# Two routed expert layers: routing work spread over more units and a third weight buffer in the first, the last layer's routing of two chunks moved one turn forward

## The reference, cut to what matters

```
# layer 0, feed-forward
n = layer_norm(x); x1 = x + n + (n @ mix_w + mix_b)
flat = layer_norm(x1); probs = softmax(flat @ router_w)        # 8 experts
topw, topi = top_k(probs, 2)
h = silu(flat @ w1[e] + b1[e]); y = h @ w2[e] + b2[e]          # e in the token's two experts
x = x1 + topw[0]*y[topi[0]] + topw[1]*y[topi[1]]

# layer 3, attention with one head
att = q @ w_in + (q * dot_scale) @ memory.T - 1e30 * mask
x = x + softmax(att) @ memory                                  # q = layernorm(x)

# layer 3, feed-forward
logits = xn @ Wg.T; top_v, top_i = top_k(logits, 2); gates = softmax(top_v)
pos = cumsum(onehot(top_i)) - 1; keep = pos < cap              # cap = 1280 per expert
inp, gate = split(xn @ W1[e]); out = (gelu(inp) * gate) @ W2[e]
x = x + the kept, gated sum of the token's two experts
```

## Time and profile before

| | us |
|---|---|
| median of 3 runs (lowest to highest) | 1486.42 (1482.06 to 1490.42) |
| the profiled execution's own time | 1486.32 |
| its span | 1484.5 |
| PE / DVE / ACT / POOL busy | 1184.3 / 991.8 / 667.6 / 537.8 |

### The profile page before, as it was taken

One profiled execution on the slowest core, in us unless ns is written; L12 is line 12 of the kernel. 1 busy time (PEld: TensorE's weight loads), 2 busy tenths in 40 slices (PEclk: granted clock), 3 DMA queues, 4 the chain that ended last, 5 costly groups with the idle time before them and its releaser, 6 DMA issues. The chain is left out here.

```text
span 1484.5 us, 34946 instructions
## 1 busy us (share of the span) xinstructions
PE 1184.3 (80%) x11154; PEld 926.2 (62%) x11154; DVE 991.8 (67%) x2920; ACT 667.6 (45%) x1423; POOL 537.8 (36%) x590
## 2 busy tenths in 40 slices
PE   2799994349899957789987879999799956399991
PEld 1577773238799934566674456677477746389991
DVE  3699885564533346989974678889477777756552
ACT  1377771115455503346554546666243343144440
POOL 2323302663305256635411233431121124752554
PEclk9999995559999966889988989999799988599996
DMA  7887733012223248534532086674200042133442
GB/s 179 211 212 196 186 105 127 29 51 65 78 79 106 85 119 205 135 100 130 155 91 51 19 191 157 152 170 106 85 1 0 0 150 64 54 119 107 147 141 74
DMA packets 138979, 164.58 MB, mean 111 GB/s; under 512 B 15309, under 2 KB 118755, under 8 KB 131729
## 3 DMA queue, kind: packets, MB, share of 16 engines
q1 hardware_dynamic: 130664, 146.62, 36.7%
q0 software_dynamic: 8192, 16.46, 4.0%
HBM read 111.98 MB, written 51.38 MB: 110 GB/s over the span
## 5 line engine op out<-in xcount | busy, mean ns | idle before, releaser
L586 DVE TENSOR_REDUCE A_neg_max<-A_s_bank 128x4 f32<-128x512 f32 x384 | 253.4, 688 | 45.0 <-PE A_s_bank L725 34.5
L448 ACT ACTIVATE A_probsT<-A_st_bank 128x512 f32<-128x512 f32 x384 | 222.2, 602 | 37.9 <-PE A_st_bank L738 36.9
L725 PE MATMUL A_s_bank<-A_k_stack,A_q_stack 72*128 72x128 bf16 x1536 | 158.9, 229 | 37.3 <-DVE A_neg_max L586 23.6
L738 PE MATMUL A_st_bank<-A_q_stack,A_k_stack 128*128 128x128 bf16 x1536 | 153.4, 224 | 7.0 <-DVE A_q_stack L602 6.2
L738 PEld LDWEIGHTS A_st_bank<-A_q_stack,A_k_stack 128*128 128x128 bf16 x1536 | 113.0, 104 | 51.7 <-issue 42.3
L725 PEld LDWEIGHTS A_s_bank<-A_k_stack,A_q_stack 72*128 72x128 bf16 x1536 | 107.2, 102 | 51.7 <-DVE A_neg_max L586 34.1
L752 PE MATMUL A_pv_bank<-A_probsT,A_v_pad 128*32 128x128 f32 x3072 | 128.3, 285 | 0.1
L2043 ACT ACTIVATE E_h<-E_h_bank,w_L_b 128x256 f32<-128x256 f32 x184 | 77.0, 472 | 82.0 <-PE E_h_bank L2143 80.8
L2143 PE MATMUL E_h_bank<-E_xT,E_w_u 128*128 128x256 f32 x368 | 91.4, 394 | 6.1 <-issue 6.1
L2155 PE MATMUL E_y_bank<-E_w,E_h 128*128 x736 | 90.3, 276 | 2.2 <-ACT E_h L2043 1.0
L752 PEld LDWEIGHTS A_pv_bank<-A_probsT,A_v_pad 128*32 128x32 f32 x3072 | 74.6, 111 | 23.5 <-issue 2.2
(11 more groups left out here) (371 smaller groups left out, 2658.5 us busy)
## 6 DMA issues: line engine op xcount, KB each, us to landing
A_q_stack<-q_scratch SPq DMA_DIRECT2D x48, 576.0 KB
A_k_stack<-k_scratch SPq DMA_DIRECT2D x32, 576.0 KB
q_scratch<-A_q_parts SPq DMA_DIRECT2D x48, 192.0 KB
A_k_stack<-k_scratch SPq DMA_DIRECT2D x48, 192.0 KB
E_xe<-slots_in SPq DMA_DIRECT2D x53, 128.0 KB
slots_out<-E_ye SPq DMA_DIRECT2D x53, 128.0 KB, 1.7
A_ctxT<-in_ctxT SPq DMA_DIRECT2D x24, 256.0 KB, 10.0
k_scratch<-A_k_parts SPq DMA_DIRECT2D x32, 192.0 KB
```

Of the source, the lines that this page charges most:

```text
L448: act.activation(probsT[n % 2][:, c * HQ:(c + 1) * HQ, :], st_bank[c % 2][:, :].rearrange("k (a q) -> k a q", a=HQ), ACT.Exp, scale=scale) ...
L586: dve.tensor_reduce(neg_max[:, c * HQ:(c + 1) * HQ], s_bank[c % 2][:, :].rearrange("q (a k) -> q a k", a=HQ), AX.X, ALU.max, negate=True). ...
L725: last = pe.matmul(s_bank[c % 2][:, a * S:(a + 1) * S], q_stack[slot][0:COMBO, h, at:at + S], k_stack[slot][0:COMBO, h, at:at + S], start= ...
L738: last = pe.matmul(dst, k_stack[slot][:, h, at:at + S], q_stack[slot][:, h, at:at + S], start=True, stop=spread)
```

## The change

`routed_ffn` (layer 0):

```diff
-    LAG = 9
+    LAG = 10
+    WBUF = 3
...
-            scatter(2, 0, 8)
+            scatter(2, 0, 12)
             inverse_deviation(3)
-            scatter(2, 8, 2 * RT)
+            scatter(2, 12, 2 * RT)
...
-                if u >= 2:
-                    dve.wait_ge(h_ready, 2 * (u - 1))
-                dve.tensor_copy(w1_u[u % 2][:, :], ...)
+                if u >= WBUF:
+                    dve.wait_ge(h_ready, 2 * (u - WBUF + 1))
+                dve.tensor_copy(w1_u[u % WBUF][:, :], ...)
...
-                    expert = {0: copy_w1(0), 1: copy_w1(1)}
+                    expert = {u: copy_w1(u) for u in range(WBUF)}
...
-                    if since == 4:
-                        add_x1(2 * c)
-                        normalise(2 * c)
-                        add_x1(2 * c + 1)
-                        normalise(2 * c + 1)
+                    if since in (4, 5):
+                        add_x1(2 * c + since - 4)
+                        normalise(2 * c + since - 4)
...
-                if u == BEGIN[NR - 1] + LAG + 1:
-                    table(1)
-                    out_rows(0)
-                if u == BEGIN[NR - 1] + LAG + 2:
-                    out_rows(1)
-                if u == BEGIN[NR - 1] + LAG + 12:
-                    out_rows(2)
-                if u == BEGIN[NR - 1] + LAG + 13:
-                    out_rows(3)
+                located = u - BEGIN[NR - 1] - LAG
+                if located in (1, 2, 3):
+                    table(1, (located - 1,))
+                if located in (4, 5, 10, 11):
+                    out_rows((4, 5, 10, 11).index(located))
```

`OneHeadFront` hooks of `capacity_ffn` (layer 3):

```diff
 POOL
-                    if b in (2, RT):
-                        inverse_root(2 if b == 2 else 3)
+                    if b in (RT, RT + 2):
+                        inverse_root(2 if b == RT else 3)
 DVE
+                if (g, half) == (3, 1):
+                    choose(0)
                 if (g, half) == (4, 0):
-                    choose(0)
+                    locate(0)
                 if (g, half) == (4, 1):
+                    dve.wait_ge(layer.x_added, START + g + 1)
                     normalise(1)
-                if (g, half) == (5, 0):
-                    locate(0)
-                if (g, half) == (6, 0):
+                if (g, half) == (5, 1):
                     choose(1)
                 if (g, half) == (6, 1):
                     dve.wait_ge(layer.x_added, START + g + 1)
+                    locate(1)
...
             statistics(3)
-            locate(1)
 ACT
-                if g in (2, 5):
+                if g in (2, 4):
                     for at in ((0, 1) if g == 2 else (2, 3)):
                         copy_xn(at)
 PE
                 if (g, half) == (3, 0):
                     logits(0)
-                if (g, half) == (3, 1):
                     logits(1)
-                if (g, half) == (4, 1):
+                if (g, half) == (4, 0):
                     count(0)
...
-                if (g, half) == (6, 1):
+                if (g, half) == (6, 0):
                     pe.wait_ge(index_done, 1)
                     count(1)
```

More of the change, by code:

```diff
@@ L1588, in routed_ffn @@
         xT = [sb(f"xT{i}", [D, UT]) for i in range(3)]
-        w1_u = [sb(f"w1_u{i}", [D, FC * 128]) for i in range(2)]
+        w1_u = [sb(f"w1_u{i}", [D, FC * 128]) for i in range(WBUF)]
         h = [sb(f"h{i}", [128, FC, UT]) for i in range(2)]
@@ L1844, in locate, with table @@
                 dve.tensor_copy(index[:, :, chunk(c)], slot[:, :, chunk(c)]).then_inc(index_done, 1)
-            def table(p):
+            def table(p, pieces=(0, 1, 2)):
                 first, last = PARTS[p]
@@ L1853, in table @@
                 hit = passed[:, 0:n, :]
[L1854 to L1881, removed]
@@ L1882, in table @@
-                dve.sem_inc(table_done, 1)
+                if 0 in pieces:
+                    own.link(dve.tensor_tensor(held[:, :], base[:, last, :], begins[:, p, :], ALU.subtract))
+                    own.did(dve.tensor_scalar(lim[:, :], held[:, :], -float(UT), 0.0, ALU.add, ALU.max))
+                    own.link(dve.tensor_tensor(square[:, :, :], held[:, :, None].to_broadcast([S, NE, MOST]),
+                                               steps[:, None, :].to_broadcast([S, NE, MOST]), ALU.is_gt))
+                    own.link(dve.tensor_reduce(units[:, :], square[:, :, :], AX.X, ALU.add))
+                    own.link(dve.tensor_tensor(square[:, :, 0:NE], upto[:, :, :],
+                                               units[:, None, :].to_broadcast([S, NE, NE]), ALU.mult))
+                    own.link(dve.tensor_reduce(ends[:, :], square[:, :, 0:NE], AX.X, ALU.add))
@@ new lines, in table @@
+                if 1 in pieces:
+                    own.link(dve.tensor_tensor(hit, per_u(ends[:, :]), per_e(numbers), ALU.is_le))
+                    own.link(dve.tensor_reduce(which[:, 0:n], hit[:, :, 0:NE - 1], AX.X, ALU.add))
+                    own.link(dve.tensor_tensor(hit, hit, per_u(ends[:, :]), ALU.mult))
+                    own.link(dve.tensor_reduce(begun[:, 0:n], hit[:, :, 0:NE - 1], AX.X, ALU.max))
+                    own.did(dve.tensor_copy(expert_of[:, at:at + n], which[:, 0:n]))
+                    own.did(dve.tensor_tensor(begun[:, 0:n], numbers, begun[:, 0:n], ALU.subtract))
@@ new lines, in table @@
+                if 2 in pieces:
+                    own.link(dve.tensor_tensor(hit, per_u(core.iota8[:, :]), per_e(which[:, 0:n]), ALU.is_equal))
+                    own.link(dve.tensor_tensor(hit, hit, per_u(lim[:, :]), ALU.mult))
+                    own.link(dve.tensor_reduce(row[:, 0:n], hit, AX.X, ALU.add))
+                    own.did(dve.tensor_scalar(which[:, 0:n], which[:, 0:n], float((last - first) * REGION),
+                                              float(first * NE * REGION), ALU.mult, ALU.add))
+                    own.link(dve.scalar_tensor_tensor(row[:, 0:n], begun[:, 0:n], float(UT), row[:, 0:n], ALU.mult, ALU.min))
+                    own.link(dve.tensor_tensor(row[:, 0:n], row[:, 0:n], which[:, 0:n], ALU.add))
+                    own.link(dve.tensor_copy(row_of[:, at:at + n], row[:, 0:n]))
+                    own.did(dve.scalar_tensor_tensor(terms[:, p, 2, :], units[:, :], float(UT), lim[:, :], ALU.mult, ALU.subtract))
+                    own.did(dve.tensor_tensor(terms[:, p, 1, :], lim[:, :], begins[:, p, :], ALU.add))
+                    own.link(dve.tensor_tensor(terms[:, p, 0, :], ends[:, :], units[:, :], ALU.subtract))
+                    own.did(dve.tensor_scalar(terms[:, p, 2, :], terms[:, p, 2, :], -float(UT), None, ALU.add))
+                    own.link(dve.scalar_tensor_tensor(terms[:, p, 0, :], terms[:, p, 0, :], float(UT), begins[:, p, :],
+                                                      ALU.mult, ALU.subtract))
+                    dve.sem_inc(table_done, 1)
@@ L1966, in _ @@
                     dve.wait_ge(w1_loaded, 16 * NE)
-                    expert = {0: copy_w1(0), 1: copy_w1(1)}
+                    expert = {u: copy_w1(u) for u in range(WBUF)}
             dve.wait_ge(b2_loaded, 16)
             for u in range(last_unit):
-                if u + 2 < last_unit:
-                    expert[u + 2] = copy_w1(u + 2)
+                if u + WBUF < last_unit:
+                    expert[u + WBUF] = copy_w1(u + WBUF)
                 copy_y(u, expert[u])
```

18 lines of the change are left out of this document (9 added, 9 removed).

## The result

The changed kernel takes 1473.23 us (median of 5 runs, 1468.89 to 1477.83), the kernel before 1486.42 beside it: a ratio of 0.9917 [0.9889, 0.9945], 13.2 us less. Forecast was 1473.0.

The account below looks back on a forecast made before the run. PE was taken to bound the last layer's units, POOL's scatters their start, and DVE's extras to stall PE in the first layer. First layer -9.3 and last layer -4.1 give -13.4 from 1486.4: 1473.0 us, range 1468 to 1481.

Parts of the forecast that it names:

- gap at unit 12 with its slow clock: First layer: PE's 6.0 us wait for DVE's weight copy and 1.7 us of slow clock both go, -7.7 us.
- turn_r, unit 4's result to unit 5's: First layer: normalising over two passes removes most of PE's 2.6 us stall, -2.2 us.
- out_rows(3)'s late weight copy: First layer, unit 24: the late weight copy is now covered, -0.2 us.
- third copy in the head: First layer's head: one more DVE weight copy delays load(0) and the count by the full 0.8 us, +0.8.
- index(0): Last layer: chunk 0's index, which starts POOL's scatters, written at 1242.55 instead of 1247.38, -4.8 us.
- POOL waits for index(1): Last layer: after chunk 0's scatters POOL waits 0.3 to 1.3 us for chunk 1's index, taken as +0.7.
- Part 1's readiness: First layer: chunk 3's later index and scatters still leave load(23) 5 us of slack, so no cost.
- Rival 1: Last layer gives little: index(1) at 1268 or later, or choose(3)/count(3) late; 1476.5 us, chance 0.16.
- The rule that I weighed and set aside: Head: DVE's fp32 copy locks the port pair shared with GpSimd; 2.5 us more lost there, sum -10.9.
- Rival 2: First layer: DVE falls behind with pieces and out_rows, PE loses about 1 us over five passes; 1478, chance 0.13.
- Rival 3: Last layer: POOL blocked at index(1), later than about 1278, makes the kernel slower; 1488 us, chance 0.04.
- Rival 4: First layer: the change doesn't reach PE, whose wait was a load or register, not DVE's copy; 1481, chance 0.07.

Follow-up runs that it names:

- head_copy_late: Changed kernel with the first layer's third weight copy moved out of the head, behind its routing; 1469.97 us, 0.9902 of the kernel before.
- last_only: Kernel before with only the last layer's part of the change, first layer as before; 1483.43 us, 0.9996 of the kernel before.
- root_early: Changed kernel with inverse_root(2) moved ahead of chunk 0's 13th scatter in the last layer; 1471.54 us, 0.9912 of the kernel before.
- spread_only: Kernel before with the first layer's extras in pieces and its moves, still two weight buffers, last layer as before; 1476.38 us, 0.9942.
- buffers_only: Kernel before with only the first layer's third weight buffer, extras whole, last layer as before; 1485.42 us, 1.0005.

## Why the prediction was right, term by term

The direction, the mechanism and the size hold, with one term that wasn't there (the third copy) and one that was left out (the scatter beside three copies). Its terms, with what the anchors gave:

| term | predicted | measured |
|---|---|---|
| gap at unit 12 with its slow clock | -7.7 | -7.8 |
| turn_r, unit 4's result to unit 5's | -2.2 | -2.2 |
| out_rows(3)'s late weight copy | -0.2 | -0.3 |
| third copy in the head | +0.8 | 0.0 (on POOL +0.8) |
| PE's start-up at unit 0, spread | not in the sum | -0.6 |
| where PE's first transpose fell in the span, spread | not in the sum | +0.8 |
| first layer in all | -9.3 | -10.2 |
| index(0) | -4.8 | -5.4 |
| POOL waits for index(1) | +0.7 | +1.3 |
| a scatter beside three copies, 1.99 less the 1.19 of before | not in the sum | +0.8 |
| last layer, to the first product | -4.1 | -3.1 |

**First layer.** Counting DVE's work in a pass against 3.4 us with three buffers and 1.8 with two was right to about 0.3 us at each place that the runs reached: the pieces alone leave the 0.64, the buffer alone leaves the 4.38. The edit of the pieces is what acts; the buffer adds 1.9 in the units and costs nothing that PE shows. The step that was mis-sized is the third copy: the prediction let load(0) slip by the full 0.8 with the scatters, and the scatters and the count do slip, but the landing that the load waits for doesn't (head_copy_late). The other two new rows are chance. The start-up: in the profiled run of the kernel before the first 16 products took 6.16 us, in the kernel after 5.53 and in last_only, with the old first layer, 5.35. And PE's first transpose stood 0.8 later in the kernel after, as much as the forecast for the third copy; 0.3 of it lies ahead of the layer's first scatter and 0.4 between that and the 17th, ahead of the copy's effect, and with the same head as the kernel before last_only has it at 331.86, later than either. The gap's price isn't the same in each execution either: in last_only, whose code is the old one there, the steps to units 12 and 13 take 16.2 us where the kernel before has 15.2.

**Part 1's readiness** was mis-sized: I had load(23) at 416.3 with 5 us to spare. SP's queue after (it takes a load each 3.73 us otherwise):

```profile
411.59 0.34 SPq L1655 DMA_DIRECT2D E_xe<-routed_in  x1
414.24 0.33 SPq L1663 DMA_DIRECT2D routed_out<-E_ye  x1
419.04 0.34 SPq L1655 DMA_DIRECT2D E_xe<-routed_in  x1
```

It comes at 419.04, 3.7 behind its turn. POOL's scatters of chunk 3 go in fours, each four behind the landing of those before, and two of these waits are 3.08 and 2.56 here instead of 1.53, so the last starts at 414.83 and not at some 413. PE wants the load in unit 20's pass, for the transposes at 422.67, and no row of it waits: the issue is 3.6 us ahead of that, where I had 7.2.

**Last layer.** The queue count of DVE and PE held to 0.1 us at its end: index(1) was forecast at 1264.3, which is 76.3 behind E3, and is written at 1250.50, 76.4 behind it. The step that was off is how far POOL would be by then: index(0) was half a us earlier than counted, and POOL was through with chunk 0 at 75.3 behind E3, where 76.0 was counted, and what index(0) gains beyond index(1) turns into waiting. root_early took that wait away by moving work into it. Rival 1 is this mechanism with index(1) at 1268.5: of its 3.6 us beyond the forecast 0.6 came.

**The rule that I weighed and set aside** held in this place, if not with its number. From the earlier trace rows I read 0.2 us as the price of three copies, because the scatter there started 0.5 us into them. Started 0.05 ahead of them it takes 1.99 and 2.00 (after, last_only), and with the copies moved off none takes over 1.21. The Trainium skill ("SBUF — State Buffer", SBUF: two separate sides) calls this an exclusive lock of the port pair that DVE and GpSimd share, held by whichever starts first. The trace agrees in that the scatter is held until the copies are through: it ends 0.85 us behind them (1265.39 and 1266.24), which is most of its own 0.97. It doesn't agree on who wins: by the profile's starts the scatter was first, and it was the one that waited.

My 2.5 us for the single copy in the head took the growth from the example of 620 and 3100 ns. The Trainium skill ("SBUF — State Buffer", A bandwidth-pool intuition that's wrong) says there that the DMA is blocked until some 115 ns behind the DVE instruction's end. By that a copy of 0.43 us would hold it up by an estimated 0.5 at most. Measured were 0.2, over ten scatters.

**The rivals.** Rival 2 didn't occur: behind three successive passes with pieces and out_rows PE has no wait. Rival 3 would have needed index(1) 14 us later than it came. Rival 4 is excluded by spread_only, whose PE gains 8.4 us with the same two buffers, by the order of the work alone. One of the signs for being right was put wrongly: it asked for the first scatter of the last layer 3.5 to 4.5 us earlier, against its own term of 4.8, and 5.4 came.

That the median was hit to 0.2 us is luck. The interval of the ratio reaches 4 us to either side, and the errors of the terms cancel: the sum held 0.8 for a third copy that PE didn't pay and 0.2 too little for the units, against 1.0 of the last layer that didn't come.

## What to carry to other kernels

Where one engine feeds another per unit, write down for each pass the work that may stand in it before the next consumer is late, and cut extras to that size. More buffers only move the wait to the next product of the same engine (buffers_only), and help once the pieces are small. A delay on one engine is a cost only if it is still there at the engine that bounds the stage: here POOL was 0.8 us late and PE's start was not (head_copy_late). When a step is brought forward, look at what the engine behind it will do once it is through: here POOL ran dry 1.3 us before the next index. A price read from one row of contention holds for its alignment only; ask what the row would be if the two had started together.

## What the hardware showed that I hadn't expected

- An indirect scatter of POOL of 0.97 us takes 1.99 to 2.00 us when three DVE copies of 128x512 fp32 (1.1 us together) start 0.05 us behind it (after, last_only, head_copy_late), 1.67 when it starts 0.26 into them (spread_only), 1.53 at 0.6 (root_early), and 1.19 at 0.5 in the kernel before. In the first three cases it ends 0.85 us behind the copies, in the last 0.5. Beside a single copy it takes 0.95 to 1.20.
- After PE waited 5.9 us its next 8 products took 3.61 us, at a granted clock of 0.51; in last_only, behind the same wait, 3.75, and the result behind them 2.58 instead of 1.95. After 4.4 us the two groups behind took 2.90 and 2.74, at 0.68 in the stretch of the first. After two waits of only 1.12 and 0.75 us a result took 3.29, at 0.60 (buffers_only), and after 0.67 and 0.76 it took 2.05, at 1.00 (before). So a shorter gap didn't save the clock's loss (1.7, 2.5, 1.8 and 1.2 us).
- A stage of unchanged code, the second attention, differs by 4.6 us between executions (261.5 to 266.1), more than the last layer's gain of 3.1. Here only anchors within a trace resolve 1 us.
